# Expert layer entry: the first pass's tokens chosen by zero-one matrices on TensorE, and slots computed from logits by doubling sums

## The reference

```python
def moe(h, gate_w, w1, w2, w3):          # E, F, TOPK = (8, 1024, 2)
    t = h.reshape(-1, hd)                # 1024 tokens of 256 features
    probs = jax.nn.softmax(t @ gate_w, axis=-1)
    topw, topi = jax.lax.top_k(probs, TOPK)
    topw = topw / jnp.sum(topw, axis=-1, keepdims=True)
    combine = jnp.zeros((T, E), t.dtype).at[jnp.arange(T)[:, None], topi].add(topw)
    up = jnp.einsum('th,ehf->etf', t, w1)
    gated = jax.nn.relu(up) * jnp.einsum('th,ehf->etf', t, w3)
    down = jnp.einsum('etf,efh->eth', gated, w2)
    out = jnp.einsum('eth,te->th', down, combine)
...
x = x + gb * _L0_ffn_ref(h, ...)         # h + attention, h + moe
```

## Time and profile before

| | |
|---|---|
| median of 3 runs | 1144.06 us (1141.77 to 1145.92) |
| the profiled execution: its own time | 1149.55 us |
| the profiled execution: span, first to last instruction | 1147.7 us |
| busy: PE, PEld, DVE, ACT, POOL | 86%, 79%, 69%, 65%, 35% |
| mean granted TensorE clock | 0.925 |
| the chain that ended last, by engine | PE 64%, DVE 15%, issue 6%, ACT 6%, DMA 3%, POOL 3% |

### The profile page before, as it was taken

The page is one execution under the profiler, slowest core; times in us unless marked ns, Lnnn a source line. Parts: engine busy times, 40 slices in busy tenths (PEclk is TensorE's granted clock), DMA queues, the critical chain, the costliest instruction groups (busy, mean ns, idle before and its releaser), DMA issues.

```text
span 1147.7 us, 22713 instructions
## 1 busy us (share of the span) xinstructions
PE 981.4 (86%) x6836; PEld 909.7 (79%) x6836; DVE 793.7 (69%) x2330; ACT 749.7 (65%) x2111; POOL 403.6 (35%) x477
## 2 busy tenths in 40 slices
PE   2567989999989899999999999999971499999982
PEld 1336989999878799988999999999971488888882
DVE  3435999889888767777776777777746256565645
ACT  1115878888878688788887888777752155555530
POOL 0333756876745533532353332222313200000022
PEclk7677999999999899999999999999995699999996
DMA  6157977987845576556556555553006355554323
GB/s 148 28 164 174 285 200 206 263 215 200 198 114 127 157 195 174 130 134 148 144 144 142 138 139 135 148 132 102 11 1 234 114 139 146 139 146 138 93 63 99
DMA packets 151820, 166.55 MB, mean 145 GB/s; under 512 B 79571, under 2 KB 108179, under 8 KB 146579
## 3 DMA queue, kind: packets, MB, share of 16 engines
q1 hardware_dynamic: 129427, 143.27, 48.2%
q10 hardware_dynamic: 20736, 17.64, 4.9%
q0 software_dynamic: 1536, 4.20, 1.1%
HBM read 106.28 MB, written 58.79 MB: 144 GB/s over the span
## 4 chain that ended last, share of the span: by engine, by line
PE 64%; DVE 15%; issue 6%; ACT 6%; DMA 3%; POOL 3%; SPq 2%; ACTq 1%; DVEq 0%; POOLq 0%
PE psO L939 14%; PE psS L906 9%; PE psX L916 8%; PE psP L838 6%; PE psY L955 6%; PE psS L1091 4%; PE psX L1091 4%; DVE pbuf L1546 2%; PE psO L1112 2%; PE psP L868 2%; PE psP L1112 2%; PE psO L922 2%; PE psP L851 2%; DVE pTl L1568 2%; DVE den L1560 1%
## 5 line engine op out<-in xcount | busy, mean ns | idle before, releaser
L1183 ACT ACTIVATE pbuf<-pbuf,nmax 128x256 f32<-128x256 f32 (+3 forms) x512 | 264.2, 518 | 39.2 <-DVE nmax L1546 38.3
L906 PE MATMUL psS<-kT,qE 128*128 128x256 f32 (+3 forms) x1024 | 238.8, 318 | 26.2 <-DVE nmax L1546 25.4
L1546 DVE CUSTOM_DVE_ANT_0 pbuf<-psS,mcau 128x256 f32<-128x256 f32 (+3 forms) x512 | 220.0, 435 | 50.5 <-PE psS L906 45.0
L1568 DVE TENSOR_TENSOR pTl<-psX,pTh 128x512 fp32r<-128x512 f32 x272 | 187.0, 688 | 71.5 <-ACT pTh L1152 70.6
L1152 ACT ACTIVATE pTh<-psX 128x512 fp32r<-128x512 f32 x272 | 160.7, 591 | 57.8 <-PE psO L939 39.8
L906 PEld LDWEIGHTS psS<-kT,qE 128*128 128x128 f32 x1024 | 162.1, 194 | 38.6 <-DVE nmax L1546 33.7
L939 PE MATMUL psO<-pTh,vpad 128*128 128x256 f32 x1088 | 186.7, 294 | 4.9 <-DVE oS L1574 3.0
L916 PE MATMUL psX<-idn,pbuf 128*128 128x128 f32 x1088 | 163.5, 276 | 6.6 <-ACT pbuf L1183 5.4
L733 POOL TENSOR_TENSOR ol<-oS,oh 128x256 fp32r<-128x256 f32 x128 | 95.0, 742 | 201.3 <-ACT oh L1152 196.8
L939 PEld LDWEIGHTS psO<-pTh,vpad 128*128 128x128 f32 x1088 | 149.7, 189 | 13.1 <-DVE oS L1574 6.7
L916 PEld LDWEIGHTS psX<-idn,pbuf 128*128 128x128 f32 x1088 | 127.8, 142 | 13.3 <-ACT pbuf L1183 5.6
(11 more groups left out here) (222 smaller groups left out, 2347.4 us busy)
## 6 DMA issues: line engine op xcount, KB each, us to landing
qd<-st SPq DMA_DIRECT2D x32, 1024.0 KB, 4.5
qE<-qd SPq DMA_DIRECT2D x128, 256.0 KB, 5.8
mrawV<-in_w_moe SPq DMA_DIRECT2D x32, 384.0 KB, 3.3
mrawB<-in_w_moe SPq DMA_DIRECT2D x32, 384.0 KB, 3.3
kT<-kd SPq DMA_DIRECT2D x64, 128.0 KB, 4.1
kT<-kd SPq DMA_DIRECT2D x32, 256.0 KB, 4.1
kd<-st SPq DMA_DIRECT2D x7, 1024.0 KB, 4.8
xg<-sq ACTq DMA_DIRECT2D x7, 640.0 KB, 5.2
```

The source lines that it names most:

```text
L906: last = mm(psS[j % 2][:, 0:n], qE[:, g % 2, j, t * P:(t + 1) * P], kT[:, g % 2, c, k0:k0 + n], start=(c == 0), stop=(c == 1))
L1183: nc.scalar.activation(pj, pj, ACT.Exp, bias=nmax[:, u % 4, j:j + 1], scale=-1.0, accum_out=sums[:, u % 4, j:j + 1]).then_inc(a_exp, 1)
L1546: V.tensor_tensor_reduce(probs(u, j), psS[j % 2][:, 0:n], mcau[:, SEQ - n:], -SCALE, 3e38, ALU.add, ALU.min, nmax[:, u % 4, j:j + 1]).then ...
L1568: V.tensor_tensor(pTl[:, kt % 2, :], psX[kt % 2][:, :], pTh[:, kt % 2, :], ALU.subtract).then_inc(v_pl, 1)
```

## The change

**Pass 0 from a product.** The 320 slots of pass 0 are filled by a product: `sel[t]` (128 tokens x 320 slots) is one where a token's lower slot equals the column number `iota`, and the sum over the tiles of features x `sel[t]` is the transposed token block of pass 0, written straight where `turn_tokens(0)` wrote it. The features are split for it: high half `fh` by ScalarE (`features_hi`), low half `fl` by GpSimd. All of these lie in `wgt_hi[1]` and `wgt_lo[1]`, expert 1's weight buffers; `iota` lies in `xin` and is doubled up by GpSimd. The scatter still runs, for the other passes; SyncE loads pass 1's slots after it.

**Slots from logits, by doubling sums.** The two experts of a token are found on the logits themselves; the running sums over 8 tiles and over 8 experts take three additions each, of shifted copies padded with zeros. Softmax, weights and `share` come after the slots.

**Work moved.** Expert 0's weights are loaded once attention is done (`s_Y`), and their low halves 0 to 5 are made by GpSimd, ahead of the scatter in its queue; VectorE keeps pieces 6 and 7, which TensorE now waits for only before the first `down`. ScalarE's `Exp` comes behind the eight `split_hi(0, q)`. `runs` grows to 4 x 12 x 8 columns, and it and the other constants are set before `hTl`.

The tile declarations, the new semaphores (`v_sel`, `a_fh`, `g_fl`, `g_iota`) and the removed lines of the old VectorE chain (L1759 to L1811) are left out below; `shares()` holds the six kinds of line that made `share` before.

```diff
@@ -275,13 +273,16 @@
         bound = sb("bound", [P, NT])
         above = sb("above", [P, NE, NT])
         ntil = sb("ntil", [P, NE])
-        base = sb("base", [P, NE + 1])
+        bases = sb("bases", [P, 4, 4 + NE])
         base_i = sb("base_i", [P, NE + 1], I32)
         wgt_hi = [sb(f"wgt_hi{i}", [P, EW], F32R) for i in range(2)]
         wgt_lo = [sb(f"wgt_lo{i}", [P, EW], F32R) for i in range(2)]
+        fh, fl = (wgt_lo[1][:, i * NT * D:(i + 1) * NT * D].rearrange("p (t d) -> p t d", t=NT) for i in range(2))
+        sel = wgt_hi[1][:, 0:NT * TP].rearrange("p (t n) -> p t n", t=NT)
         mrawV = sb("mrawV", [P, EV])
         mrawB = sb("mrawB", [P, EV])
         xin = sb("xin", [P, XT, D])
+        iota = xin[:, :, :].rearrange("p j d -> p (j d)")[:, 0:TP]
         relu_s = sb("relu_s", [P, 2, TP])
         gated = sb("gated", [P, 2, TP])
         ysbT = sb("ysbT", [P, KC, TP])
...
@@ -650,12 +655,16 @@
                 else:
                     step_causal(u)

-            sp.wait_ge(s_ht, TB)
+            sp.wait_ge(s_Y, NU)
             sp.dma_start(before_s[:, :], before).then_inc(ld_before, 16)
             load_expert(0, range(NPC))
             sp.wait_ge(v_slot, 1)
             for e in range(1, NE):
                 load_expert(e, range(NPC))
+                if e == 1:
+                    sp.wait_ge(v_sel, NT)
+                    sp.wait_ge(st_xg, 16 * 2 * NT)
+                    sp.dma_start(xin[:, :, :], xg[TP:TP + XT * P, :].rearrange("(j p) d -> p j d", p=P)).then_inc(ld_xg, 16)
             for t in range(NT):
                 sp.wait_ge(v_out, t + 1)
                 sp.dma_start(out[t // TB, t % TB * P:(t % TB + 1) * P, :], xN[:, t, :]).then_inc(st_res, 16)
@@ -780,6 +789,27 @@
             low_wq(2)
             for u in range(NU + 5):
                 step(u)
+
+            pool.wait_ge(s_Y, NU)
+            link(G.tensor_copy(iota[:, 0:NE], ids[:, :]))
+            n = NE
+            while n < TP:
+                m = min(2 * n, TP)
+                last = G.tensor_scalar(iota[:, n:m], iota[:, 0:m - n], float(n), None, ALU.add)
+                if m < TP:
+                    link(last)
+                else:
+                    last.then_inc(g_iota, 1)
+                n = m
+            for t in range(NT):
+                pool.wait_ge(a_fh, t + 1)
+                apart(pool)
+                G.tensor_tensor(fl[:, t, :], rows_of(t), fh[:, t, :], ALU.subtract).then_inc(g_fl, 1)
+            for q in range(NPC - 2):
+                pool.wait_ge(w_hi, q + 1)
+                apart(pool)
+                at = slice(q * PC, (q + 1) * PC)
+                G.tensor_tensor(wgt_lo[0][:, at], raw_piece(q), wgt_hi[0][:, at], ALU.subtract).then_inc(w_lo, 1)

             pool.wait_ge(v_slot, 1)
             pool.wait_ge(st_zero, 16 * 15)
...
@@ -1072,7 +1102,7 @@

             def turn_tokens(i):

-                wait(pe, ld_xg, 16 * (i + 1))
+                pe.wait_ge(ld_xg, 16 * i)
                 wait(pe, a_yo, i)
                 wait(pe, v_yo, i)
                 for k in range(KC):
@@ -1115,9 +1145,12 @@

             def begin(e, first):

-                ready = NPC * first + NPC if e else NPC
-                pe.wait_ge(w_hi, ready)
-                pe.wait_ge(w_lo, ready)
+                if e:
+                    pe.wait_ge(w_hi, NPC * first + NPC)
+                    pe.wait_ge(w_lo, NPC * first + NPC)
+                else:
+                    pe.wait_ge(w_hi, NPC - 2)
+                    pe.wait_ge(w_lo, NPC - 2)
                 apart(pe)

             def one(e, i):
@@ -1133,6 +1166,9 @@
                     if f == 0:
                         turn_output(i)
                     else:
+                        if e == 0 and f == 1:
+                            pe.wait_ge(w_hi, NPC)
+                            pe.wait_ge(w_lo, NPC)
                         down(e, i, f - 1)
                 turn_tokens(i + 1)
                 down(e, i, NF - 1).then_inc(m_dn, 1)
@@ -1142,7 +1178,14 @@
                 last = mm(psD[m][:, 0:TP], idn[:, :], hb[:, 0:2, :].rearrange("p t d -> p (t d)")[:, 0:TP],
                           start=True, stop=True)
             last.then_inc(m_dn, 1)
-            turn_tokens(0)
+            for t in range(NT):
+                pe.wait_ge(v_sel, t + 1)
+                pe.wait_ge(g_fl, t + 1)
+                for k in range(KC):
+                    for n, a in enumerate((fh, fl)):
+                        last = mm(psTr[k][:, 0:TP], a[:, t, k * P:(k + 1) * P], sel[:, t, :],
+                                  start=(t == 0 and n == 0), stop=(t == NT - 1 and n == 1))
+            last.then_inc(s_x, 1)
             experts(pe, begin, one)
             turn_output(first_pass_of(pe, NE))

@@ -1386,13 +1429,20 @@
                 else:
                     step_causal(u)

+            def features_hi(t):
+                act.wait_ge(v_h, 4 * TB + t + 1)
+                copy(fh[:, t, :], rows_of(t)).then_inc(a_fh, 1)
+
             root(6, 1)
+            act.wait_ge(s_Y, NU)
+            for t in range(TB):
+                features_hi(t)
             for t in range(TB, NT):
                 act.wait_ge(s_ht, t - TB + 1)
                 copy(hTh[:, :, t * P:(t + 1) * P], psX[t % 2][:, 0:D].rearrange("p (k n) -> p k n", k=KC)).then_inc(a_hth, 1)

-            act.wait_ge(v_lmax, 1)
-            nc.scalar.activation(pr[:, :, :], logit[:, :, :], ACT.Exp).then_inc(a_rt, 1)
+            for t in range(TB, NT):
+                features_hi(t)

             def split_hi(e, q):

@@ -1404,10 +1454,11 @@
                 act.dma_start(xin[:, :, :], xg[bass.ds(i * TP, XT * P), :].rearrange("(j p) d -> p j d", p=P))\
                    .then_inc(ld_xg, 16)

-            def tokens_hi(i):
+            def tokens_hi(i, load=True):

                 act.wait_ge(s_x, i + 1)
-                load_tokens(i + 1)
+                if load:
+                    load_tokens(i + 1)
                 for k in range(KC):
                     last = copy(xTh[:, k, :], psTr[k][:, 0:TP])
                 last.then_inc(a_x, 1)
@@ -1450,14 +1501,14 @@

             for q in range(NPC):
                 split_hi(0, q)
-            act.wait_ge(st_xg, 16 * 2 * NT)
-            load_tokens(0)
-            tokens_hi(0)
+            act.wait_ge(v_lmax, 1)
+            nc.scalar.activation(pr[:, :, :], logit[:, :, :], ACT.Exp).then_inc(a_rt, 1)
+            tokens_hi(0, load=False)
             experts(act, begin, one)
             tiles = first_pass_of(act, NE)
             output(tiles)
             store(tiles)
-            act.wait_ge(ld_xg, 16 * (tiles + 2))
+            act.wait_ge(ld_xg, 16 * (tiles + 1))
             apart(act)


@@ -1740,18 +1791,65 @@
             finish_root(6, at)
             for t in range(TB, NT):
                 expert_features(t)
+            link(V.memset(runs[:, :, :, :], 0.0))
+            link(V.memset(bases[:, :, :], 0.0))
+            link(V.memset(bound[:, 0:1], -1.0))
+            for k in range(1, NT):
+                last = V.memset(bound[:, k:k + 1], float(k * TP))
+            link(last)
             for t in range(TB, NT):
                 dve.wait_ge(a_hth, t - TB + 1)
                 V.tensor_tensor(hTl[:, :, t * P:(t + 1) * P], psX[t % 2][:, 0:D].rearrange("p (k n) -> p k n", k=KC),
                                 hTh[:, :, t * P:(t + 1) * P], ALU.subtract).then_inc(v_htl, 1)

             dve.wait_ge(s_rt, NT)
-            parts = psS[0][:, 0:NT * 2 * NE].rearrange("p (t c e) -> p t c e", c=2, e=NE)
-            link(V.tensor_copy(logit[:, :, :], parts[:, :, 0, :]))
-            link(V.tensor_tensor(logit[:, :, :], logit[:, :, :], parts[:, :, 1, :], ALU.add))
-            link(V.tensor_reduce(lmax[:, :], logit[:, :, :], mybir.AxisListType.X, ALU.max))
-            link(V.tensor_tensor(logit[:, :, :], logit[:, :, :], lmax[:, :].unsqueeze(2).broadcast_to([P, NT, NE]),
-                                 ALU.subtract), v_lmax)
+            parts = psS[0][:, 0:NT * 2 * NE].rearrange("p (t c e) -> p t e c", c=2, e=NE)
+            link(V.tensor_reduce(logit[:, :, :], parts, mybir.AxisListType.X, ALU.add))
+            for t in range(NT):
+                last = V.max(top[:, t, :], logit[:, t, :])
+            link(last)
+            for t in range(NT):
+                last = V.max_index(topi[:, t, :], top[:, t, :], logit[:, t, :])
+            link(last)
+            link(V.tensor_copy(topf[:, :, :], topi[:, :, :]))
+            for i in range(2):
+                last = V.tensor_tensor(cc[:, i, :, :], ids[:, :].unsqueeze(1).broadcast_to([P, NT, NE]),
+                                       topf[:, :, i:i + 1].broadcast_to([P, NT, NE]), ALU.is_equal)
+                link(last)
+            link(V.tensor_tensor(picked[:, :, :], cc[:, 0, :, :], cc[:, 1, :, :], ALU.add), v_pick)
+
+            dve.wait_ge(s_rank, 1)
+            link(V.tensor_copy(runs[:, 0, 4:4 + NT, :], psP[:, 0:NT * NE].rearrange("p (t e) -> p t e", e=NE)))
```

(40 more changed lines are left out.)

60 lines of the change are left out of this document (13 added, 47 removed).

## The result

The changed kernel takes 1125.14 us (median of 4 runs, 1123.61 to 1127.67) against 1142.91 of the kernel before (4 runs, 1140.96 to 1145.92): a ratio of 0.9844, 95% interval 0.9815 to 0.9874. That is 17.8 us faster; the forecast was 10.1, to 1134.0. It lies in the stated range, but the gain is three quarters larger than the forecast. The same two kernels on a later chip were 15.4 us apart (1142.6 and 1127.22, experiment 9), so the gain itself is known to some 2 us.

What follows compares the result with a forecast made beforehand. Bound: the entry's serial chain, features and logits, VectorE's small operations, then the tokens' detour through DRAM; later passes run at TensorE's pace. -6.8 + (30.05 - 11.55) - 1.6 = 10.1 earlier, 1144.06 to 1134.0 us; range 1123 to 1139.

Steps and rivals of the forecast that it cites:

- Features and logits, 2.75 later: Before the logits: VectorE's feature operations wait for GpSimd's subtractions (2.1 us), memsets add 0.55, ScalarE 0.1; 2.75 us later.
- The chain, 4.5 shorter: VectorE from logits to slots: fewer small operations and softmax moved back take 8.3 us in place of 12.8.
- 8.6 longer by the subtractions: Logits to slots: GpSimd's six 1.84 us weight subtractions each hold one VectorE operation, making slots 8.6 us later.
- Slots to the first product, 10.3 to 12.8: Selection by 32 products replaces scatter and read back: 10.3 to 12.8 us from slots to first product, not 30.05.
- The start of pass 0, 1.6 lost: First product to `turn_output`: VectorE's subtractions, shares, loop bounds and copy take 4.95 us against TensorE's 3.36; 1.6 lost.
- Covered: Scatter and load of pass 1's slots end at 908.5, before pass 1's transposes at 920.8: 12 us of cover.
- The rival of a slower scatter: Scatter calls slowed by VectorE in pass 0 become the bound; at 3.1 us a call, 1148 us; chance 0.03.
- The sum, 10.1: All entry terms together: the kernel 10.1 us faster, between 8.8 and 11.3 by the clock.
- the engines hardly meet: Entry: VectorE mostly slips past GpSimd's subtractions, both delays vanish, 20.5 us gained, 1123.6; chance 0.24 including meeting half.

Runs made afterwards that it cites:

- experiment 9: The changed kernel run again unaltered on a later chip, for a second profile: 1127.22 us.
- experiment 1: The changed kernel with low halves 0 to 5 of expert 0's weights back on VectorE, behind the softmax: 1121.55 us.
- experiment 5: The kernel before with only the new slot chain, zero fills, and softmax and shares after the slots: 1141.6 us.
- experiment 8: The changed kernel with the eight operations of the shares moved from pass 0's entry to the end of the last pass: 1124.86 us.
- experiment 6: The changed kernel with 33 memsets on GpSimd between the wait for the slots and the scatter, to make it late: 1139.64 us.
- experiment 12: The kernel before with six filler products on TensorE at the end of every pass: 1138.26 us.
- experiment 3: The kernel before with twelve filler products on TensorE at the end of every pass: 1141.57 us.
- experiment 4: The changed kernel with twelve filler products on TensorE at the end of every pass: 1128.94 us.
- experiment 2: The changed kernel with GpSimd's feature subtractions waiting until VectorE has made all features: 1125.68 us.
- experiment 7: The changed kernel, entry reordered: low halves on VectorE, feature subtractions waiting, fills and `psD` product later, softmax and shares at the end: 1114.67 us.
- experiment 10: The kernel of experiment 7 with six filler products on TensorE at the end of every pass: 1111.5 us.

## Why the prediction was right and wrong

The mechanism of the entry was right: the scatter and the read back leave the path, the engines take turns where GpSimd subtracts, and what `turn_output` gains is still there at pass 1. Two things made the sum too small. The entry's terms were mis-sized, above all the turns with GpSimd (8.6, measured 6.7) and slots to the first product (10.3 to 12.8, measured 9.8), so that 10.1 stands for 13.4; and the passes behind the entry were put at nothing, though their clock was not the same on both sides, which is worth 2.0 to 3.4 more by the profiles. Point by point, by its steps:

- **Features and logits, 2.75 later.** 2.33 measured (8.83 less 6.50): 1.42 at the four `hb`, as 3.09 stands in place of 1.67, and 0.89 for the fills. They alternate as forecast, but three of the four last 0.95, not near 1.1. So the meeting was priced 0.7 too high and the fills 0.3 too low.
- **The chain, 4.5 shorter.** 4.4 (12.6 to 8.2), shown by experiments 1 and 5.
- **8.6 longer by the subtractions.** 6.7. Five operations were held, not six: `topf`, two marks, `picked`, one of the three additions, each to GpSimd's 1.77 a piece. GpSimd also began earlier against VectorE's chain than I had placed it, so that `topf` met only half an operation. Forecast of a taking of turns, with 1.3 to 1.9 an operation: right but for `topf`'s 0.86. Slots came 4.6 later than before, not 6.8.
- **Slots to the first product, 10.3 to 12.8.** 9.8, below the range. The clock was expected to rise some 5.4 us after the product that opens the selection; it stood at 0.67 in the stretch from 880.5 and at 1.00 from 882, some 3.5 us after TensorE began at 877.99. So the 32 products took 5.22, not 6.0 or more.
- **The start of pass 0, 1.6 lost.** 2.4 lost (5.8 in place of 3.4). I had put the reading of the bounds at 0.85, and it took 1.91, since the linked shares stand ahead of it (experiment 8). The shares thus cost some 3.4 of VectorE, not 1.6.
- **Covered.** The scatter took 1.26 a call with the gap behind it, a few calls more, 1.33 in the mean against 1.38 before; the load of pass 1 was issued at 901.10, and the cover is 10.5 us (experiment 6). I had 12, from a load issued at 905.6; the load was sooner, but so was pass 1. The rival of a slower scatter fails. The Trainium skill ("SBUF — State Buffer", section "SBUF: two separate sides") had stood for it. Of the two calls beside the eight `sel` the first takes 1.22, as the first call of before does, and the other 0.96, the same as beside an idle VectorE; the longest, 1.43, stands beside a subtraction of weights, though another call beside one takes 0.96.
- **The sum, 10.1.** The terms above give 13.4: 0.4 at the logits, 2.0 from there to the slots and 1.8 from the slots to the first product came better, 0.8 at the start of pass 0 came worse. Nothing was wrong in kind here; three sizes were off toward the careful side and one was not.
- **What had no term: TensorE's clock.** The prediction took the passes as equal on both sides, and the rows of before held the reason against it: passes 1 to 5 took 27.4 to 27.5 us, pass 6 26.0. The profiles of the changed kernel have two and three low starts fewer, which left 2.0 and 3.4 us over passes 1 to 6 after its longer odd passes. With the 13.4 of the entry and pass 0's 0.6, which has no term either, that is 16.0 to 17.4, where the medians give 17.8 and 15.4. It is an account by single profiles: the median of before has some three low starts, by experiment 12, and profile and median differ by up to 4.6 us in experiment 6. That the passes count is shown by experiments 3, 4 and 12. Why a pass start falls in one kernel more often than in another isn't settled, nor whether the change itself makes low starts rarer (experiments 1 and 2 have none, 6 has three): only that it can fall where TensorE idles twice at a pass's end, and didn't where one of the gaps is filled.

The rival "the engines hardly meet" (1123.6) comes nearest in its number and is wrong in its cause: experiment 1 is that case, and its entry is 4.2 us shorter than the changed kernel's. A number so near the measured one would here have stood on a wrong reason.

## What to carry to other kernels

A chain of small operations with two SBUF inputs on VectorE should have no queue of GpSimd subtractions beside it: where both queues are full, price each such operation at GpSimd's whole duration (1.74 us for 0.24 here), and count how many fall into the queue's time. When work is taken out of a stretch, ask what the engine does next with the time: the doubling sums saved 4.4 us and, beside the product, nearly nothing (35.43 and 35.08). With the softmax and the shares gone from the place behind the slots, and the fills, `fl` and the product for `psD` moved too, `turn_output` came at 26.85; how much of that belongs to each of these moves wasn't tested. And before a gain is put at the entry alone, list the durations of the loop's passes: where they come in two sizes, a term is missing.

## What the runs showed of the hardware

- **A short idle at a loop's seam can cost more than itself.** TensorE idles 0.8 and then 0.85 to 0.97 us at a pass's end, with 1.15 us of work between. Where the granted clock fell there (to the 1.2 GHz level, 0.57 to 0.62 in the mean of 4 us), the pass took 1.4 us more. Six products of 0.147 in the second gap kept it at 2.4 GHz at every pass start in the profiles of two kernels, for nothing in the pass's length, and took 4.3 us off the kernel before.
- **Not held by GpSimd's subtractions:** `MAX8` and `FIND_INDEX8` (0.64 us for eight, and 0.16 each), the reduction of the logits out of PSUM (0.29), the copy out of PSUM (0.23), and in experiment 2 the feature subtraction with one input in PSUM. A `CAST` of 64 columns from uint32 in SBUF was held (0.85 in place of 0.20). The Trainium skill ("SBUF — State Buffer", section "Who interferes with whom") names casts among those that can be held, and frees an operation with at most one input in SBUF outside its two-port modes; the trace agrees.
- **Reading the loop bounds cost nothing behind two long subtractions and 1.9 us behind linked short operations** (experiment 8: 1.91 idle, then none).
- **TensorE kept the high clock into pass 0 in experiments 7 and 10,** where the product for `psD` follows the selection and 0.77 us of idle stand ahead of the first product (experiment 7): `turn_output` followed it after 2.2 us. In the changed kernel, with 1.85 idle, the clock fell during the first 12 products (0.147 each at first, then 0.267), and `turn_output` followed after 5.8, of which 2.8 is the wait for VectorE. That the shorter idle is the cause was not tested by itself.
